# Second feed-forward: one TensorE signal per pass, stages two passes further apart, routing weights copied by VectorE

## The reference

```python
g = jnp.einsum('th,eih->eti', x, gate_proj)
u = jnp.einsum('th,eih->eti', x, up_proj)
inter = jax.nn.silu(g) * u
expert_out = jnp.einsum('eti,ehi->eth', inter, down_proj)
sel = expert_out[topk_idx, jnp.arange(T)[:, None]]
y = jnp.einsum('tkh,tk->th', sel, topk_weight)
shared_out = jax.nn.silu(sg) * su @ shared_down_w.T
return y + shared_out
```

## Time and profile before

| | us |
|---|---|
| timed, median of 3 runs | 1418.01 (1416.52 to 1421.49) |
| profiled execution, span from first to last instruction | 1481.7 |
| second feed-forward in it, from the first up matmul | 1029 to 1481.7 |
| busy in the span: PE, DVE, ACT, POOL | 1190.4, 911.7, 784.9, 516.5 |

### The profile page before, as it was taken

One profiled execution on the slowest core, in us unless ns is written; L12 is line 12 of the kernel. 1 busy time (PEld: TensorE's weight loads), 2 busy tenths in 40 slices (PEclk: granted clock), 3 DMA queues, 4 the chain that ended last, 5 costly groups with the idle time before them and its releaser, 6 DMA issues. The chain is left out here.

```text
span 1481.7 us, 27979 instructions
## 1 busy us (share of the span) xinstructions
PE 1190.4 (80%) x9258; PEld 1081.2 (73%) x9258; DVE 911.7 (62%) x2119; ACT 784.9 (53%) x2205; POOL 516.5 (35%) x585
## 2 busy tenths in 40 slices
PE   2776249997899999999999999975898767778674
PEld 1555139887799998888888888875887766667563
DVE  3887645552666666678657787766876322234667
ACT  2776115552566667665657665554654433345442
POOL 3566033553000001100354005543634555654442
PEclk9676559998999999999999999997999878889897
DMA  7753224553722000100233003443844545444896
GB/s 139 206 173 125 81 84 136 153 151 76 199 65 66 8 2 22 30 8 2 69 112 107 16 3 128 129 146 112 285 125 144 154 150 154 150 129 147 284 285 224
DMA packets 139588, 177.13 MB, mean 120 GB/s; under 512 B 22048, under 2 KB 120512, under 8 KB 139456
## 3 DMA queue, kind: packets, MB, share of 16 engines
q1 hardware_dynamic: 110752, 122.57, 28.8%
q0 software_dynamic: 17792, 43.14, 9.0%
q10 hardware_dynamic: 10912, 9.70, 1.9%
HBM read 107.28 MB, written 68.09 MB: 118 GB/s over the span
## 5 line engine op out<-in xcount | busy, mean ns | idle before, releaser
L1690 ACT ACTIVATE attend_s<-attend_s,attend_less 128x128 f32<-128x128 f32 x512 | 198.3, 392 | 108.4 <-DVE attend_less L1831 99.9
L2331 POOL DMA_INDIRECT answers<-ahead_plain,moe_dst x160 | 157.4, 984 | 186.5 <-ACT ahead_plain L2410 97.5
L1643 POOL TENSOR_TENSOR router_xn<-rest_acc,router_mv 128x512 f32<-128x512 f32 x12 | 12.7, 1058 | 426.6 <-DVE router_rs L1294 372.3
L81 PE MATMUL moe_psU<-moe_wh,moe_xl 128*128 (+1 forms) x384 | 118.1, 308 | 4.3 <-issue 3.3
L2477 DVE TENSOR_TENSOR moe_it<-moe_it,moe_psU 128x256 f32<-128x256 f32 x96 | 40.2, 418 | 128.9 <-ACT moe_it L2392 82.6
L83 PE MATMUL moe_psU<-moe_wh,moe_xh 128*128 (+1 forms) x384 | 115.9, 302 | 3.3 <-issue 3.2
L82 PE MATMUL moe_psU<-moe_wl,moe_xh 128*128 (+1 forms) x384 | 116.5, 303 | 2.3 <-issue 2.2
L1262 POOL DMA_INDIRECT slots<-router_row,router_idx x80 | 81.0, 1013 | 93.9 <-DMA router_row<-normed_rows 62.2
L1708 ACT ACTIVATE attend_pt<-attend_psS 128x1024 f32<-128x1024 f32 x64 | 65.5, 1024 | 83.2 <-PE attend_psS L1982 82.0
L1829 DVE SCALAR_TENSOR_TENSOR attend_s<-attend_psS,held_bias 128x1024 f32<-128x1024 f32 x64 | 78.0, 1219 | 44.3 <-PE attend_psS L1975 44.2
L2640 PE MATMUL moe_psI<-const_ident,moe_it 128*128 128x128 f32 x192 | 42.1, 305 | 78.4 <-DVE moe_il L2473 68.0
(11 more groups left out here) (384 smaller groups left out, 4175.6 us busy)
## 6 DMA issues: line engine op xcount, KB each, us to landing
ahead_plain<-slots SPq DMA_DIRECT2D x160, 129.0 KB
moe_both<-answers SPq DMA_DIRECT2D x28, 512.0 KB
router_row<-normed_rows SPq DMA_DIRECT2D x40, 256.0 KB
layer_raw<-in_wi_dram SPq DMA_DIRECT2D x8, 1024.0 KB, 4.8
layer_raw<-in_wo_dram SPq DMA_DIRECT2D x8, 1024.0 KB, 6.8
slots<-router_xn SPq DMA_DIRECT2D x4, 2048.0 KB, 11.0
ahead_plain<-in_gex_dram SPq DMA_DIRECT2D x17, 384.0 KB
moe_both<-normed_rows SPq DMA_DIRECT2D x24, 256.0 KB
```

The costliest lines, as they stand in the source:

```text
L81: pe.matmul(out, wl, mh, start=first, stop=False)
L1690: last = nc.scalar.activation(s[:, g, j, :], s[:, g, j, :], ACT.Exp, bias=less[:, g, j:j + 1], accum_out=sm[:, g, j:j + 1])
L2331: nc.gpsimd.indirect_dma_start(out=R.YT[q], out_offset=bass.IndirectOffsetOnAxis(ap=dst[:, r % NM, s:s + 1], axis=0), in_=yb[:, r % NY, s, ...
```

## The change

TensorE's order in a pass becomes turn(j+2), up(j), down(j-4), turn_inner(j-2), and only the last of them signals, on one semaphore `passed`. All waits on TensorE's results become waits for the end of the pass in which the result was made. The loop has 100 passes instead of 98. ScalarE's order is i_high(j-2), x_high(j+2), silu(j), y_out(j-4); VectorE's is i_low(j-2), x_low(j+2), inner(j), targets(j+2), add(j-4), then the extra work as before. The routing weights are copied by VectorE in `targets`, the ring of targets and weights has 12 places, and the loads of answers start two steps later.

```diff
-    NT, NS, NM = 2, 4, 8
+    NT, NS, NM = 2, 4, 12
+    TURN_AHEAD, INNER_BEHIND, DOWN_BEHIND = 2, 2, 4
+    PASSES = PAIRS_ALL + DOWN_BEHIND
+        def pass_over(eng, j):
+            eng.wait_ge(passed, j + TURN_AHEAD + 1)
+        def turn_done(eng, j):
+            pass_over(eng, j - TURN_AHEAD)
+        def up_done(eng, j):
+            pass_over(eng, j)
+        def inner_done(eng, j):
+            pass_over(eng, j + INNER_BEHIND)
+        def down_done(eng, j):
+            pass_over(eng, j + DOWN_BEHIND)
-        answered_from = STARTS_OF[1] + NX + 4
+        answered_from = STARTS_OF[1] + NX + 4 + DOWN_BEHIND - 2
             def x_high(j):
-                act.wait_ge(t_done, j + 1)
+                turn_done(act, j)
+                if j >= 2:
+                    up_done(act, j - 2)
-            def weighted(j):
-                r = NTH[j]
-                act.wait_ge(x_in[j % NX], x_count(j))
-                if r >= NM:
-                    act.wait_ge(y_up, r - NM + 1)
-                nc.scalar.activation(wd[:, r % NM, :], xg[:, j % NX, :, D], ACT.Copy).then_inc(g_up, 1)
             def y_out(j):
-                act.wait_ge(y_done, j + 1)
-                act.wait_ge(g_up, r + 1)
+                down_done(act, j)
+                act.wait_ge(d_up, r + 1)
             def targets(j):
+                v.tensor_copy(wd[:, r % NM, :], xg[:, j % NX, :, D])
@@ TensorE
-            for j in range(PAIRS_ALL + 2):
+            for j in range(PASSES):
+                if j + TURN_AHEAD < PAIRS_ALL:
+                    last = turn(j + TURN_AHEAD)
                 if j < PAIRS_ALL:
-                    up(j, bases[j])
+                    last = up(j, bases[j])
+                if j >= DOWN_BEHIND:
+                    last = down(j - DOWN_BEHIND, bases.pop(j - DOWN_BEHIND))
+                if 0 <= j - INNER_BEHIND < PAIRS_ALL:
+                    last = turn_inner(j - INNER_BEHIND)
+                last.then_inc(passed, 1)
                 if j + 1 < PAIRS_ALL:
                     bases[j + 1] = bases_of(j + 1)
-                if j + 2 < PAIRS_ALL:
-                    turn(j + 2)
-                if 1 <= j <= PAIRS_ALL:
-                    turn_inner(j - 1)
-                if j >= 2:
-                    down(j - 2, bases.pop(j - 2))
```

More of the change, by code:

```diff
@@ L2130, in moe @@
         sent = [sem(f"sent{k}") for k in range(NS)]
-        w_hi, w_early, w_late, t_done, x_hi, x_lo, u_done, s_up, i_up, i_done, i_hi, i_lo, y_done, y_up, d_up, g_up = (
-            sem(n) for n in ("w_hi", "w_early", "w_late", "t_done", "x_hi", "x_lo", "u_done", "s_up", "i_up", "i_done", "i_hi", "i_lo", "y_done", "y_up", "d_up", "g_up"))
+        w_hi, w_early, w_late, passed, x_hi, x_lo, s_up, i_up, i_hi, i_lo, y_up, d_up = (
+            sem(n) for n in ("w_hi", "w_early", "w_late", "passed", "x_hi", "x_lo", "s_up", "i_up", "i_hi", "i_lo", "y_up", "d_up"))
         made, r_done, r_free, col_up, table_up, marked, c_up, c_step, stored, added, aside_up = (
@@ L2217, in load @@
                 if j >= NX:
-                    sp.wait_ge(t_done, j - NX + 1)
+                    turn_done(sp, j - NX)
                     if not is_shared(j - NX):
                         sp.wait_ge(d_up, NTH[j - NX] + 1)
-                        sp.wait_ge(g_up, NTH[j - NX] + 1)
                 if is_shared(j):
@@ L2382, in x_high @@
             def x_high(j):
-                act.wait_ge(t_done, j + 1)
+                turn_done(act, j)
+                if j >= 2:
+                    up_done(act, j - 2)
                 nc.scalar.activation(xh[:, j % 2, :], psX[j % 2][:], ACT.Copy).then_inc(x_hi, 1)
             def i_high(j):
-                act.wait_ge(i_done, j + 1)
+                inner_done(act, j)
                 nc.scalar.activation(ih[:, j % 2], psI[:, 0:N], ACT.Copy).then_inc(i_hi, 1)
             def silu(j):
-                act.wait_ge(u_done, j + 1)
+                up_done(act, j)
                 nc.scalar.activation(it[:, j % 2], psU[j % 2][:].rearrange("p (s n) -> p s n", s=2)[:, :, 0:I1], ACT.Silu).then_inc(s_up, 1)
-            def weighted(j):
-                r = NTH[j]
-                act.wait_ge(x_in[j % NX], x_count(j))
-                if r >= NM:
-                    act.wait_ge(y_up, r - NM + 1)
-                nc.scalar.activation(wd[:, r % NM, :], xg[:, j % NX, :, D], ACT.Copy).then_inc(g_up, 1)
             def y_out(j):
                 r = NTH[j]
-                act.wait_ge(y_done, j + 1)
-                act.wait_ge(g_up, r + 1)
+                down_done(act, j)
+                act.wait_ge(d_up, r + 1)
                 if r >= NY:
@@ L2415, in _ @@
             x_high(1)
-            for j in range(PAIRS_ALL + 2):
+            for j in range(PASSES):
+                if 0 <= j - INNER_BEHIND < PAIRS_ALL:
+                    i_high(j - INNER_BEHIND)
+                if j + TURN_AHEAD < PAIRS_ALL:
+                    x_high(j + TURN_AHEAD)
                 if j < PAIRS_ALL:
                     silu(j)
-                if j + 2 < PAIRS_ALL:
-                    x_high(j + 2)
-                    if not is_shared(j + 2):
-                        weighted(j + 2)
-                if 1 <= j <= PAIRS_ALL:
-                    i_high(j - 1)
-                if j >= 2 and not is_shared(j - 2):
-                    y_out(j - 2)
+                if j >= DOWN_BEHIND and not is_shared(j - DOWN_BEHIND):
+                    y_out(j - DOWN_BEHIND)
                 for k in (2 * j + 1, 2 * j + 2):
@@ L2479, in add @@
             def add(j):
-                dve.wait_ge(y_done, j + 1)
+                down_done(dve, j)
                 a = rows(acc[:, 2 * NTH[j]:2 * NTH[j] + 2, :])
@@ L2555, in _ @@
             R.aggregate(dve, LAST, stat3)
-            for j in range(PAIRS_ALL + 2):
+            for j in range(PASSES):
+                if 0 <= j - INNER_BEHIND < PAIRS_ALL:
+                    i_low(j - INNER_BEHIND)
+                if j + TURN_AHEAD < PAIRS_ALL:
+                    x_low(j + TURN_AHEAD)
                 if j < PAIRS_ALL:
                     inner(j)
[L2559 to L2566, removed]
+                if j + TURN_AHEAD < PAIRS_ALL and not is_shared(j + TURN_AHEAD):
+                    targets(j + TURN_AHEAD)
+                if j >= DOWN_BEHIND and is_shared(j - DOWN_BEHIND):
+                    add(j - DOWN_BEHIND)
                 for k in (2 * j + 1, 2 * j + 2):
@@ L2609, in turn @@
                         last = nc.tensor.transpose(psX[j % 2][:, k * N + s * P:k * N + (s + 1) * P], xg[:, j % NX, s, k * P:(k + 1) * P], C["ident"][:])
-                last.then_inc(t_done, 1)
+                return last
             def bases_of(j):
@@ L2632, in up @@
                                        [part(w, bases[s], k * 2 * I1, 2 * I1) for w in (wh, wl)], k == 0, k == KD - 1)
-                last.then_inc(u_done, 1)
+                return last
             def turn_inner(j):
@@ L2640, in turn_inner @@
                     last = nc.tensor.transpose(psI[:, s * P:(s + 1) * P], it[:, j % 2, s, :], C["ident"][:])
-                last.then_inc(i_done, 1)
+                return last
             def down(j, bases):
@@ L2650, in down @@
                                    [part(w, bases[s], 4 * I1, D) for w in (wh, wl)], True, True)
-                last.then_inc(y_done, 1)
+                return last
             split(pe, 0)
-            turn(0)
-            turn(1)
+            turn(0).then_inc(passed, 1)
+            turn(1).then_inc(passed, 1)
             bases = {0: bases_of(0)}
-            for j in range(PAIRS_ALL + 2):
+            for j in range(PASSES):
                 if j == STARTS_OF[0]:
```

## The result

The kernel after takes **1432.97 us**, median of 4 runs (1428.69 to 1435.16), against 1418.59 (1416.52 to 1421.49) for the kernel before beside it: ratio 1.0092, 95% interval 1.0066 to 1.0119, so slower by 14.4 us. The prediction was 1425.7, slower, range 1396 to 1434, so the time is 1.0 us inside its upper end.

The account below looks back on a forecast made before the run. It took GpSimd (POOL, 3.95 us per pass) to bound pairs 26 to 57 and the chain of answers the end. Terms 5.6 + 2.4 - 1.4 + 0.7 + 0.4 = +7.7 us on 1418.0 gave 1425.7 us, range 1396 to 1434.

Parts of the forecast that it names:

- start, the first twelve passes: Crowded first passes: the looser order lets VectorE work ahead up to a pass; -1.4 us, bounds -2.8 to 0.
- fill, up(12) to the first scatter: y_out comes two passes later, so the first scatter does too and POOL keeps the delay; +5.6 us, bounds 0 to 7.9.
- rows of the second part, 57 to 67: Pair 68's rows load only after all sends land, so POOL idles near pair 62; +2.4 us, bounds 0 to 3.9.
- VectorE's copies, 67 to 91: 80 small weight copies move to VectorE and cost time in the 18 passes with answers; +0.7 us, at most 2.7.
- end: After the last answer: a shorter chain, -1.1 us, but two shared pairs' adds move behind answers; net +0.4 us.
- Fewer signals: TensorE's four updates per pass become one, 288 fewer; gain 0.
- Waiting for the end of the pass: ScalarE starts after the pass; cost 0 while a signal is less than 1.1 us late.
- The reading of the 63.7 us: Profiled span exceeds the timed median by 63.7 us; a good part could be late TensorE signals, few in timed runs.
- thinner signals arrive in time: Rival, chance 0.20: TensorE's late signals go away, saving 32 us in the send passes; 1386, or 1402 for half.
- words stay late: Rival, chance 0.08: signals stay late and now everything waits for one, +31 us over pairs 12 to 79; 1449.
- TensorE pays for each update: Rival, chance 0.08: three fewer updates per pass give 6.5 us on TensorE; 1411.5 with the fill hidden.
- Nothing: Rival, chance 0.20: POOL has gaps in timed runs, the two passes are caught up, the rest under 2 us; 1418.

Follow-up runs that it names:

- after_again: The kernel after, unchanged, profiled a second time; 1429.63 us (one run).
- before_again: The kernel before, unchanged, profiled a second time; 1418.00 us (one run).
- copy_only: The kernel before with only the routing weights copied by VectorE and rings of 12 places; 1418.86 us, ratio 0.9995.
- four_signals: The kernel after, but each of TensorE's four steps signals on its own semaphore and all waits go back to these; 1432.64 us, ratio 1.0104.
- deep_own: The kernel after's depth with four signals, up ahead of turn, ScalarE's and VectorE's order of before, a third inner-row buffer; 1427.46 us, ratio 1.0075.
- x_first_four: The kernel after with four signals, and x_high ahead of i_high, x_low ahead of i_low; 1430.35 us, ratio 1.0065.
- one_signal: The kernel before in its own order and depth, with one signal at a pass's end that all engines wait for; 1435.51 us, ratio 1.0121.

## Why the prediction held, and where its terms were off

The forecast was the likeliest of its cases, and the part of its mechanism that carries most of its sum is what the runs show: GpSimd sets pairs 26 to 57, so what is lost in front is kept, and more is lost when the rows of pair 68 come late. Its size was about half, and that 1432.97 lies inside 1396 to 1434 is in part luck. Added up, the terms' own bounds give 1415.6 to 1432.9 (the text has 1417 to 1433), so the time stands at their upper end, and two terms, the start and the rows, came out beyond their bounds. Term by term (measured: mean of after and after_again against the mean of before_again and copy_only):

| term | predicted, bounds | measured |
|---|---|---|
| start, the first twelve passes | -1.4 (-2.8 to 0) | +4.6 |
| fill, up(12) to the first scatter | +5.6 (0 to 7.9) | +7.1 |
| pairs 12 to 57 | 0 | +0.3 |
| rows of the second part, 57 to 67 | +2.4 (0 to 3.9) | +4.6 |
| VectorE's copies, 67 to 91 | +0.7 (0 to 2.7) | -0.3 |
| end | +0.4 | +0.3 |
| sum | +7.7 | +16.6; timed 14.4 |

The 2.2 us between the measured sum and the timed difference are within what two profiled executions of one kernel differ by (1433.0 and 1427.8 for after).

- *Fewer signals: 0.* Right: four_signals equals after. Where nothing is waited for, after's passes are 2.78 us apart (1087.18 and 1089.96), 2.79 before. The prediction counted 288 updates fewer; they are 282, from 384 to 102. The Trainium skill's increment of about 26 ns ("TensorE: Matmul & The Clock Gate", on the per-tile semaphore tail) would be an estimated 0.08 us a pass and some 7.5 us in all. No run here shows it: four_signals and after are 0.3 us apart.
- *Start: -1.4.* This is the term that was most wrong, 6 us and the sign. It said that the looser order lets VectorE work ahead in the crowded first passes; instead TensorE stands longer before the router's steps and works at a lower clock. Not settled is how much of the +4.6 belongs to the order, the depth and the wait for the end: deep_own and x_first_four, which wait less, stand at 56.6 and 57.0, between 53.9 and 58.5, and a difference of 1.9 us is seen without any cause.
- *Waiting for the end of the pass: cost 0.* It counted the slack of x_low and i_low, 1.1 us and more, and held that y_out "ends within the pass". It didn't ask who waits for the work that stands last in the queues, and the router's steps and the first scatter do. one_signal prices the wait at 17.5 us when there is no depth to cover it. With the depth of after no run isolates it: after's ratio is 1.0092 and deep_own's 1.0075, with intervals that overlap. In pairs 12 to 26 the depth buys it back (45.4 us against 52.4).
- *Two passes more: +5.6.* Right as far as it went: +4.9 up to the end of down. The 2.3 us of y_out's new place, behind the inner transposes and three steps of ScalarE, weren't in the sum.
- *Rows of pair 68: +2.4.* The chain was the right one, and the sum of its steps was short. From the last send (1278.07) the load was issued 3.65 us later (4.5 taken), the rows took 3.49 (3 taken), the pass, up to the end of its inner transposes, 4.70 (2.8 taken), y_out 1.92 (2.2 taken), and 0.76 us lie between the answers' copy and its scatter (0 taken): 14.5 in place of 12.5. The pass was long for a reason that the sum didn't have, the clock, below.
- *Copies and end.* Small, as said. The answers are 3.67 us apart in after too (1319.50 to 1403.92, 23 steps).
- *The reading of the 63.7 us.* Taken on trust and right: the late words are absent in before_again.

Of the rivals, "thinner signals arrive in time" and "words stay late" both rested on late words, which the ordinary execution hardly has. "TensorE pays for each update" fell with four_signals. "Nothing" fell because GpSimd's gaps lie ahead of pair 26, where TensorE is busy 42.02 of 45.40 us and GpSimd 27.16, so that nothing is caught up.

## What to carry to other kernels

In this kernel a single signal for a pass gives TensorE nothing; its price is that every step of the other engines begins at the pass's end (17.5 us in one_signal). Ask who waits for what stands last in their queues: side work that TensorE wants next, and the output that another engine waits for. Depth hides that in the steady part and is paid as fill, in full where a later engine has no gaps. Look for that engine first, and give it its work earlier, as the sends two passes sooner do (4.7 us). And before a trace is argued from, its span is held against the timed runs: one that is 4.5% long has stalls of its own.

## What the runs showed that wasn't expected

**Late words of one execution.** In the profiled execution of the front, ScalarE waited 51.0 us with no releaser known before silu, and 68.0 us of TensorE's time went for i_low. The same kernel again has no such wait of ScalarE, and for TensorE from 1027.5 on

```profile
PE moe_psI L2640 <- DVE moe_il L2473: 48.4, 26, 5.3
```

In that first execution the median time from the end of a signalling TensorE instruction to its semaphore's record was 2.7 us between 1150 and 1200; in before_again, after, after_again, one_signal and four_signals it is 0.014 us, with at most three over 1 us in the whole stage, the longest 8 us. As before_again is the same kernel, neither the number of signals nor the order makes it. What does stays open.

**The clock after a wait.** TensorE's long wait for pair 68 has a price beyond its length. Windows of after, the columns as above:

```profile
1263.00:1276.00 13.00, 12.96 (x113) 12.72 (x111) 7.76 (x25) 8.55 (x24) 9.98 (x15) 1.00 0.48 151
1276.00:1285.20 9.20, 0.00 (x0) 0.00 (x0) 1.58 (x5) 1.87 (x5) 7.07 (x8) 0.65 0.41 134
1285.20:1288.50 3.30, 3.29 (x16) 3.29 (x17) 0.00 (x0) 0.00 (x0) 2.39 (x4) 0.50 0.73 195
1288.50:1292.00 3.50, 3.50 (x30) 3.50 (x30) 1.57 (x5) 1.87 (x5) 0.72 (x1) 0.93 0.68 192
```

TensorE was full at 1.00 (2.4 GHz), stood 9.2 us, and did its next 16 matmuls in 3.3 us at 0.50 (1.2 GHz) before the clock came back. Half of 3.3 us, and a little of the next stretch, is the 1.8 us by which this pass was longer, 4.70 us from its first transpose to the end of its inner ones against 2.94 for the pass that began at 1273.02. The same stretch of before_again, with 1.4 us of wait, stays at 1.00.
